# Message stage of a graph layer: one-hot rows, squares and an addition change engines

## What is computed

```python
x_tangent = logmap0(x)
x_local_tangent = logmap(x[row], x[col])
cat = jnp.concatenate([x_tangent[row], x_tangent[col], distances], axis=-1)
h = jax.nn.silu(cat @ att_w1 + att_b1)
att = jax.nn.sigmoid(h @ att_w2 + att_b2) * edge_mask
agg = jax.ops.segment_sum(x_local_tangent * att, row, num_segments=N) / NORM_FACTOR
```

```python
def mink_dot(x, y):
    return -x[..., 0:1] * y[..., 0:1] + jnp.sum(x[..., 1:] * y[..., 1:], axis=-1, keepdims=True)
def logmap(x, y):
    xy = jnp.clip(mink_dot(x, y) + K, None, -EPS) - K
    u = y + xy * x * C
    normu = jnp.clip(mink_norm(u), MIN_NORM, None)
    dist = jnp.sqrt(sqdist(x, y))
    return proj_tan(dist * u / normu, x)
```

## Time and profile before

| | us |
|---|---|
| median of 3 runs | 4663.93 (4658.82 to 4669.4) |
| the profiled execution, its own time | 4658.17 |
| its span, first to last instruction | 4656.4 |
| busy in the span: PE / DVE / ACT / POOL | 3060.8 / 3660.8 / 2576.1 / 2040.5 |
| mean granted clock of TensorE | 0.853 |

### The profile page before, as it was taken

The page is one execution under the profiler, slowest core; times in us unless marked ns, Lnnn a source line. Parts: engine busy times, 40 slices in busy tenths (PEclk is TensorE's granted clock), DMA queues, the critical chain, the costliest instruction groups (busy, mean ns, idle before and its releaser), DMA issues. The chain is left out here.

```text
span 4656.4 us, 64180 instructions
## 1 busy us (share of the span) xinstructions
PE 3060.8 (66%) x12512; PEld 2411.7 (52%) x12513; DVE 3660.8 (79%) x10698; ACT 2576.1 (55%) x5409; POOL 2040.5 (44%) x2519
## 2 busy tenths in 40 slices
PE   1101111566878778877745788888888888888686
PEld 0101111454656555655534676766666766676554
DVE  6879998555999999999964677777777777787666
ACT  0013332003555555555554688887878787878655
POOL 1000000005777777777500655655655555556201
PEclk9965555777999999999978899989999999899887
DMA  0010001326887787878655665655655655565441
GB/s 7 0 37 0 0 0 39 80 76 196 243 239 238 242 243 237 242 239 243 186 130 112 186 163 160 164 155 156 164 162 157 165 158 160 155 164 162 106 92 44
DMA packets 294461, 663.96 MB, mean 143 GB/s; under 512 B 77025, under 2 KB 146335, under 8 KB 293869
## 3 DMA queue, kind: packets, MB, share of 16 engines
q0 software_dynamic: 141312, 463.51, 35.0%
q1 hardware_dynamic: 152813, 197.32, 15.5%
HBM read 615.78 MB, written 44.88 MB: 142 GB/s over the span
## 5 line engine op out<-in xcount | busy, mean ns | idle before, releaser
L1812 POOL DMA_INDIRECT big<-d_qv,at_col x880 | 934.7, 1062 | 568.0 <-DMA at_col<-by_dst_edge_cols 288.9
L2225 POOL DMA_INDIRECT big<-d_xr,ms_col x528 | 528.4, 1001 | 617.4 <-DMA ms_col<-by_src_edge_cols 260.5
L2302 PE MATMUL ms_near_a<-big,ms_hotT 128*128 x1760 | 575.0, 410 | 37.5 <-ACT ms_hotT L2352 20.7
L2303 PE MATMUL ms_near_c<-big,ms_hotT 128*128 x1760 | 563.2, 403 | 0.0
L1858 PE MATMUL at_out<-at_pv,at_hot 128*128 128x264 f32 x1760 | 518.2, 420 | 4.6 <-DVE big L2024 3.1
L1838 PE MATMUL at_kx<-big 128*128 x1760 | 498.8, 410 | 32.3 <-ACT big L1912 23.1
L2225 POOL DMA_INDIRECT ms_more<-d_xr,ms_col x352 | 355.9, 1011 | 228.9 <-PE ms_out L2322 155.8
L2322 PE MATMUL ms_out<-big,ms_hot 128*128 128x257 f32 x1056 | 317.3, 427 | 188.6 <-ACT ms_hot L2387 187.7
L2302 PEld LDWEIGHTS ms_near_a<-big,ms_hotT 128*128 128x128 f32 x1760 | 361.9, 207 | 105.1 <-issue 44.7
L1838 PEld LDWEIGHTS at_kx<-big 128*128 128x128 f32 x1760 | 352.7, 205 | 113.0 <-issue 54.2
L2303 PEld LDWEIGHTS ms_near_c<-big,ms_hotT 128*128 128x128 f32 x1760 | 362.3, 206 | 61.7
(11 more groups left out here) (370 smaller groups left out, 7038.7 us busy)
## 6 DMA issues: line engine op xcount, KB each, us to landing
big<-by_dst_marks SPq DMA_DIRECT2D x110, 512.0 KB, 5.4
ms_hotT<-by_src_marks SPq DMA_DIRECT2D x110, 448.0 KB
big<-d_qv,at_col POOLq DMA_INDIRECT x880
d_qv<-big SPq DMA_DIRECT2D x5, 2240.0 KB, 9.1
big<-d_xr,ms_col POOLq DMA_INDIRECT x528
ms_hotT<-by_src_marks SPq DMA_DIRECT2D x110, 60.0 KB
ms_more<-d_xr,ms_col POOLq DMA_INDIRECT x352
d_xr<-mid_hm SPq DMA_DIRECT2D x5, 1124.4 KB, 12.4
```

The costliest lines, as they stand in the source:

```text
L1812: pool.indirect_dma_start(out=ring[t.slot][:, k, :], out_offset=None, in_=m.d_qv, in_offset=bass.IndirectOffsetOnAxis(ap=col[:, t.h, k, 0: ...
L2225: pool.indirect_dma_start(out=far[t.slot][:, k, :], out_offset=None, in_=m.d_xr, in_offset=bass.IndirectOffsetOnAxis(ap=col[:, t.h, k, 0:1 ...
L2302: TE.matmul(near_a[:, (SPAN * p + k) % 4, 0:TW], rows, m.tab_a[:, bass.ds(at, TW)], start=True, stop=True)
L2303: last = TE.matmul(near_c[:, p % 2, k * DIM:(k + 1) * DIM], rows, m.tab_c[:, bass.ds(at, DIM)], start=True, stop=p % 2 == 0)
```

## The change

The node term is stored twice in a row of `d_xr` (columns 256 and 257; a row is now 514 words). DVE adds near_a to 257 columns, the term among them, and `angles` takes the near term as the sum less the second copy; the separate copy is gone. PE adds the gathered MLP half by identity for all pairs, so ACT's silu always reads `near_c` and DVE's addition is gone. The squares move from DVE to ACT. The one-hot columns are made by DVE with one `is_equal`, the one-hot rows, weighted at once by c, with one `is_equal, mult` per tile; ACT's passes for both are gone, and `hot` has one buffer. PE's sums come one pair later; POOL's gathers come one pair later too, `place_a` and `finish` standing after the first and second of a turn. The product of `attention_sums` is written in place.

```diff
-XW = DIM + 1 + DIM
+XB = DIM + 2
+XW = XB + DIM
...
-                    ln.mark(V.tensor_copy(hm[:, g % 2, :, DIM], m.kept_mink[:, at]))
+                    ln.mark(V.tensor_copy(hm[:, g % 2, :, DIM:XB], bcast(m.kept_mink[:, at], XB - DIM)))
...
-        hot = sb("hot", [P, 2, G, P])
+        hot = sb("hot", [P, G, P])
...
             def _(pool):
...
                 def period(t):
                     w = window_of(t)
+                    gather_pair(t.plus(1), 3)
+                    gather_pair(t.plus(2), 0)
                     if w:
                         place_a(w)
-                    gather_pair(t.plus(2), 0)
                     gather_pair(t.plus(2), 1)
                     if w:
                         finish(w)
                     gather_pair(t.plus(2), 2)
-                    gather_pair(t.plus(2), 3)
...
             def _(pe):
...
                     if before.exists():
                         pe.wait_ge(apart, before.n * SG + q + 1)
-                        if p % 2:
-                            pe.wait_ge(silu_in, before.n * SG + q + 1)
-                        else:
-                            pe.wait_ge(v_in, before.n * (SG // 2) + q // 2 + 1)
-                    if p == 1:
+                        pe.wait_ge(silu_in, before.n * SG + q + 1)
+                    if p == 0:
                         pe.wait_ge(got[t.slot], t.turns(RING) * (16 * G))
                     for k in range(SPAN):
...
-                        last = TE.matmul(near_c[:, p % 2, k * DIM:(k + 1) * DIM], rows, m.tab_c[:, bass.ds(at, DIM)], start=True, stop=p % 2 == 0)
-                        if p % 2:
-                            last = TE.matmul(near_c[:, p % 2, k * DIM:(k + 1) * DIM], m.ident[:, :], far[t.slot][:, SPAN * p + k, TW:XW],
-                                             start=False, stop=True)
+                        TE.matmul(near_c[:, p % 2, k * DIM:(k + 1) * DIM], rows, m.tab_c[:, bass.ds(at, DIM)], start=True, stop=False)
+                        last = TE.matmul(near_c[:, p % 2, k * DIM:(k + 1) * DIM], m.ident[:, :], far[t.slot][:, SPAN * p + k, XB:XW],
+                                         start=False, stop=True)
...
-                        sums(old, p)
+                        sums(*pair_before(old, p, 1))
                         near(t if p < 2 else t.plus(1), (p + 2) % SG)
...
             def _(act):
...
+                def squares(t, p):
...
+                    act.wait_ge(apart, t.n * SG + p + 1)
+                    for k in range(SPAN):
...
+                        AC.activation(junk[:, k, 1:DIM], far[t.slot][:, SPAN * p + k, 1:DIM], ACT.Square,
+                                      accum_out=SQ[:, t.wslot, at:at + 1]).then_inc(squared, 1)
...
                     silu(t, 0)
-                    scale(old, 0)
-                    hot_columns(t.plus(1), 0)
-                    hot_columns(t.plus(1), 1)
+                    squares(t, 0)
                     silu(t, 1)
-                    scale(old, 1)
                     if w:
                         chain(w)
+                    squares(t, 1)
                     silu(t, 2)
-                    scale(old, 2)
-                    hot_rows(t.plus(-LAG + 1))
+                    squares(t, 2)
                     silu(t, 3)
-                    scale(old, 3)
+                    squares(t, 3)
...
             def _(dve):
...
-                    V.tensor_copy(OWN[:, t.wslot, k0:k0 + SPAN], near_a[:, bank:bank + SPAN, DIM]).then_inc(copied, 1)
-                    near = far[t.slot][:, SPAN * p:SPAN * p + SPAN, 0:DIM]
-                    V.tensor_tensor(near, near, near_a[:, bank:bank + SPAN, 0:DIM], ALU.add).then_inc(apart, 1)
-                    if p % 2 == 0:
-                        rows = far[t.slot][:, SPAN * p:SPAN * p + SPAN, TW:XW]
-                        V.tensor_tensor(rows, rows, near_c[:, p % 2, :].rearrange("p (k d) -> p k d", d=DIM), ALU.add).then_inc(v_in, 1)
...
+                    near = far[t.slot][:, SPAN * p:SPAN * p + SPAN, 0:TW]
+                    V.tensor_tensor(near, near, near_a[:, bank:bank + SPAN, 0:TW], ALU.add).then_inc(apart, 1)
+
+                def hot_columns(t):
...
+                    dve.wait_ge(bc_in[t.h % 2], t.turns(2) * 48)
+                    V.tensor_scalar(part, part, m.lane[0:ROWS, 0:1], None, ALU.is_equal).then_inc(hotT_in, 1)
+
+                def hot_rows(t, p):
...
+                    if p == 0:
+                        dve.wait_ge(c_ready, t.window + 1)
+                    if t.plus(-1).exists():
+                        dve.wait_ge(out_in, t.plus(-1).n * SG + p + 1)
+                    for k in (SPAN * p, SPAN * p + 1):
+                        at = (t.h % WG) * G + k
+                        V.tensor_scalar(hot[:, k, :], m.ramp[:, :], col[:, t.h, k, 1:2].bitcast(F32), cs[:, t.wslot, at:at + 1],
+                                        ALU.is_equal, ALU.mult).then_inc(weighted, 1)
...
                         ln.mark(V.tensor_tensor(Q[:, k], rows[:, :, 0], rows[:, :, 0], ALU.mult))
-                        ln.mark(V.tensor_tensor(E[:, k], rows[:, :, DIM], own[:, k], ALU.add))
+                        ln.mark(V.tensor_tensor(own[:, k], rows[:, :, DIM], rows[:, :, DIM + 1], ALU.subtract))
...
                     for p in range(SG):
                         differences(t, p)
+                        attention_sums(*pair_before(t, p, 1))
                         if p == 0 and w:
                             angles(w)
-                        squares(t, p)
-                        attention_sums(*pair_before(t, p, 1))
+                        if p == 1:
+                            hot_columns(t.plus(1))
+                        done, q = pair_before(old, p, 2)
+                        if done.exists():
+                            add(done, q, starts.values(q, 1)[0])
...
+                        hot_rows(old, p)
```

More of the change, by code:

```diff
@@ L2321, in sums @@
                         j = SPAN * p + k
-                        last = TE.matmul(out[:, p % 2, 0:TW], hot[:, t.h % 2, j, :], far[t.slot][:, j, 0:TW], start=(k == 0), stop=(k == SPAN - 1))
+                        last = TE.matmul(out[:, p % 2, 0:TW], hot[:, j, :], far[t.slot][:, j, 0:TW], start=(k == 0), stop=(k == SPAN - 1))
                     last.then_inc(out_in, 1)
@@ L2339, in _ @@
                 act.wait_ge(made, 2)
[L2341 to L2352, removed]
                 def silu(t, p):
@@ L2365, in hot_rows @@
-                def hot_rows(t):
+                    rows = far[t.slot][:, SPAN * p:SPAN * p + SPAN, XB:XW]
+                    act.wait_ge(near_in, t.n * SG + p + 1)
+                    AC.activation(rows, near_c[:, p % 2, :].rearrange("p (k d) -> p k d", d=DIM), ACT.Silu).then_inc(silu_in, 1)
+                def squares(t, p):
                     if not t.exists():
                         return
-                    act.wait_ge(col_in[t.h], (t.i + 1) * 16)
-                    if t.plus(-2).exists():
-                        act.wait_ge(out_in, t.plus(-2).n * SG + SG)
-                    for k in range(G):
-                        AC.activation(hot[:, t.h % 2, k, :], m.ramp[:, :], ACT.Abs, scale=-1.0,
-                                      bias=col[:, t.h, k, 1:2].bitcast(F32)).then_inc(far_rows, 1)
-                    act.wait_ge(far_rows, t.n * G + G)
-                    AC.activation(hot[:, t.h % 2], hot[:, t.h % 2], ACT.Relu, scale=-1.0, bias=one).then_inc(hot_in, 1)
@@ L2378, in scale @@
-                def scale(t, p):
-                    if not t.exists():
-                        return
-                    if p == 0:
-                        act.wait_ge(c_ready, t.window + 1)
-                        act.wait_ge(hot_in, t.n + 1)
-                    for k in (SPAN * p, SPAN * p + 1):
-                        c = cs[:, t.wslot, (t.h % WG) * G + k:(t.h % WG) * G + k + 1]
-                        AC.activation(hot[:, t.h % 2, k, :], hot[:, t.h % 2, k, :], ACT.Copy, scale=c).then_inc(scaled, 1)
+                    act.wait_ge(apart, t.n * SG + p + 1)
@@ L2447, in squares @@
-                def squares(t, p):
+                    near = far[t.slot][:, SPAN * p:SPAN * p + SPAN, 0:TW]
+                    V.tensor_tensor(near, near, near_a[:, bank:bank + SPAN, 0:TW], ALU.add).then_inc(apart, 1)
+                def hot_columns(t):
                     if not t.exists():
                         return
-                    dve.wait_ge(apart, t.n * SG + p + 1)
-                    k0 = (t.h % WG) * G + SPAN * p
-                    before, q = pair_before(t, p, 2)
-                    for k in range(SPAN):
-                        if before.exists():
-                            dve.wait_ge(al_in, before.n * G + SPAN * q + k + 1)
-                        row = far[t.slot][:, SPAN * p + k, 1:DIM]
-                        V.tensor_tensor_reduce(out=junk[:, k, 1:DIM], in0=row, in1=row, scale=1.0, scalar=0.0, op0=ALU.mult, op1=ALU.add,
```

(7 more changed lines are left out.)

85 lines of the change are left out of this document (35 added, 50 removed).

## The result

The changed kernel takes **4738.3 us** (median of 4 runs, 4721.9 to 4746.0) against 4666.7 for the kernel before beside it: ratio 1.0151, 95% interval 1.0117 to 1.0186. The forecast was 4630. That is above the upper end of the range, 4725. Slower was the side of rival 2, but not by its terms: it gave 4715.

A forecast was written before the change was run, and what follows sets the result against it. Bound: loops of PE, ACT and POOL waiting on each other, no full engine. Per window 27.7 + 0.7 + 2.1 + 0.9 + 0.9 = 32.3 us against 32.9; 54 windows with prologue and drain -34 us: 4630 us, range 4530 to 4725.

The forecast's parts named there:

- rival 2: Message stage: the wait for the last gather pair decides, PE restarts at 1.2 GHz each window; 33.9 us, 4715; chance 0.23.
- Landing: Turn's last gather, from its end on POOL until PE can use it: 2.7 us (2.4 to 2.9); PE idles 2.1 more.
- E: Count's zero: end of issue of PE's sum releasing the gather before the finish; PE wants the last gather at E + 14.6.
- PE's products: PE, message stage: identity products for all pairs make 64 products per window, 27.7 us, 3.5 more than before.
- Silu's wait: PE waits for ACT's silu of pair 2, delayed by the chain and two squares: 0.7 us per window (0.4 to 0.8).
- The clock: PE restarting at 1.2 GHz after idling for gathers costs 1.8 us; half charged, 0.9 per window (0 to 1.8).
- the loop's 0.9: Engines take up their loop anew once per five windows: 0.9 us per window, expected to stay.
- POOL's path: From E through two gathers and the finish (5.6 us) to the end of the turn's last gather, E + 13.9.
- c_ready's cover: The finish on POOL reaches DVE's weighted rows before PE needs them, with 0.7 us of cover: no cost.
- Prologue and drain: Ends of the message stage: +2 us for turn 0's gathers wanted earlier, -4 for last sums not awaiting ACT.
- Rival 1: Message stage: gathers land in time and only silu's wait is left; 29.3 us per window, 4470, half-way 4550; chance 0.20.
- Rival 4: DVE's one-hot instructions stop POOL through their shared port: 35.8 us per window, 4820; chance 0.05.

The follow-up runs named there:

- e4: The changed kernel with SyncE issuing the marks' transfer one pair of PE later: 4571.2 us against 4662.0 for the kernel before, ratio 0.9806.
- e2: The changed kernel with the angle chain's finish on DVE instead of POOL: 4451.5 us against 4662.0 for the kernel before, ratio 0.9551.

## Why the prediction was wrong, step by step

**The step that failed** is one term: "Landing: ... 2.9 us after its end, under heavier transfers; I take 2.7 (2.4 to 2.9). Landed at E + 16.6." It measured 5.5, E + 19.6, in the window shown, and 5.1 on average. The row I took it from the earlier trace rows has nothing but gathers in flight. In the 3 us of that landing, 2569.7 to 2572.7 us of the kernel before, the DMA queues show one line alone:

```profile
q0 software_dynamic: 190, 0.64, 74.5%
```

The hardware queue, which brings the marks, moved no packet there; I called it the heavier case without looking at who shared the engines. I had SyncE's queue down as "its wait is unchanged: nothing". Its wait is unchanged, but the change moved the turn's last gather, and PE's need for it, onto the same moment, which made that transfer part of the path. e4 shows it. As a mechanism "a wait for the last gather pair" was right; its size was off, 4.3 us per window (4.56 in the one shown) instead of 2.1.

The window's account after: 64 products x 0.432 = 27.6; gathers 4.3; silu and differences (6.0 + 5.4 + 4.4 + 2.2) / 28.9 = 0.6; the remainder to 34.6, clock and loop, 2.1. Forecast: 27.7, 2.1, 0.7, 1.8. The gathers' term alone is 2.2 us of the 2.3 between 32.3 and 34.6. 54 x 2.3 = 124 us stand against a miss of 88 + 34 = 122 between the profiled executions; between the medians it is 108.

- **PE's products:** right. **Silu's wait:** (5.4 + 4.4) / 28.9 = 0.3 us, forecast 0.7, and as much again for DVE's differences, which I had not counted.
- **The clock:** I charged half of 1.8. The 12 instructions after the stall took 4.43 us on average of the 28 windows, 1.8 more than at full clock; so 0.3 is left of the remainder, and the loop's 0.9 can't be seen apart. At stalls of the forecast's size e4 paid in seven windows of 31, less than half.
- **POOL's path:** right. Finish 3409.46 to 3414.95, 5.5 us with its wait (5.6); last gather E + 14.1 (13.9).
- **DVE:** hot columns 751 ns (0.75), hot rows 269.8 / 880 = 0.31 us each (0.27), 0.6 us more per window, and beside other work.
- **ACT:** a square every 0.4 us (0.5 at most).
- **c_ready's cover:** held: PE waited 5.9 us in the whole stage for weighted rows.
- **Prologue and drain:** 0 and 88 - 92 = -4 us, forecast +2 and -4.
- **The signs:** PE's wait for the gathers once per window came, and none for the weighted rows. "POOL's waits for PE shorter than now" did not: 150 + 116 us in 1000 instead of 134 + 89, since PE's stall holds back the sums that release the gathers (one wait of 6.71 us behind the stall in the window shown). Nor did rival 2's granted clock below 0.90: it was 0.94 from 3000 to 4000 us.
- **Rival 1** (29.3 us) named the prize rightly, and e2's earlier gathers, which it names as a way, reach it; the change as made does not. **Rival 2** had its direction right, and the full clock cost; its price stopped at 2.8 us of idle because the landing's upper end was 2.9. **Rival 4** (the shared port) did not come on the average, 1.01 us per gather as before; see below.

What stays open: why 64 columns still cost 0.6 us of landing. A marks transfer placed ahead of the gathers instead of behind them was not tried. Why a start only 0.75 us after the gather's end delays nothing is not shown either.

## What to carry to other kernels

When a change moves a consumer's wait, look up everything that is released around the same moment, transfers of other queues too: two things paced by one engine's steps keep their distance, and here met in 24 windows of 28. A landing time read while one queue runs alone is a lower bound, not a middle; take as upper end one with the other queue's bytes in flight. And where a stall of a few us comes once per period, try moving waits or issues by one step before any arithmetic is moved: here that took 246 us off.

## What the runs showed that I had not expected

**A transfer of another queue in front of a gather.** With 512 KB from SyncE's queue starting beside the gather's end (0.64 us before to 0.27 after), its landing goes from 3.0 (e4) to 5.4 us on average. The Trainium skill (DMA: Bandwidth & Descriptors, section "Queues, rings and completion order") says that each DMA engine takes turns between its queues packet by packet; the 56% and 37% shares above and the landing that grows with the marks agree.

**The port, after all, but for one shape.** Of 456 gathers from 3000 to 4000 us of the changed kernel, laid beside DVE's timeline, 399 that did not overlap the 127x1024 one-hot columns took 0.97 us on average (at most 1.25), those among them beside the 128x128 weighted rows about 0.99. The 57 that did took 1.27: 35 of them 1.35 to 1.49, while the column instruction itself kept to 0.75, and 20 the usual 0.94 or 0.95, while in 18 of these the column instruction took 0.80 to 0.82. Such a pair:

```profile
3416.20 0.75 DVE L2410 TENSOR_SCALAR ms_hotT<-ms_hotT,lane 127x1024 f32<-127x1024 f32 x1
```

and the gather of 3416.30 above, 1.47 us for 0.95. It lies on POOL's path to the last gather; the forecast's bound of 0.25 us per gather was too low for this one. The Trainium skill (SBUF — State Buffer, section "SBUF: two separate sides") would have DVE's single-source instruction hold the port; the column instruction agrees with at most 0.55 us, the weighted rows show next to none of it.
